# Cross-attention and expert stage: context loaded transposed as well, Wq and Wk folded, keys' low parts on GpSimd

## What is computed

```python
x = x + attention(layernorm(x), ctx)        # ctx: 4 x 1601 x 128
#   Q = ln(x) Wq + bq;  K = ctx Wk + bk;  V = ctx Wv + bv
#   softmax(clip(Q K^T / sqrt(128), -100, 100)) V
x = x + experts(layernorm(x))               # 8 experts, hidden 256, top 2 by router
```

## Time and profile before

| | us |
|---|---|
| median of 3 runs | 165.13 |
| lowest, highest | 164.04, 165.61 |
| span of the profiled execution, first to last instruction | 162.5 |

### The profile page before, as it was taken

One profiled execution on the slowest core, in us unless ns is written; L12 is line 12 of the kernel. 1 busy time (PEld: TensorE's weight loads), 2 busy tenths in 40 slices (PEclk: granted clock), 3 DMA queues, 4 the chain that ended last, 5 costly groups with the idle time before them and its releaser, 6 DMA issues. The chain is left out here.

```text
span 162.5 us, 2919 instructions
## 1 busy us (share of the span) xinstructions
PE 153.8 (95%) x932; PEld 134.7 (83%) x932; DVE 126.0 (78%) x330; ACT 105.9 (65%) x215; POOL 35.8 (22%) x36
## 2 busy tenths in 40 slices
PE   7779999999999999999999989989999999999983
PEld 7569887889989989888869867778888888887872
DVE  0789996496976578177387799899899979977794
ACT  3178785747484636727586745788798798888550
POOL 1292000000120030010063670333323323333020
PEclk9999999999999999999999999999999999999999
DMA  4999960000000000000000000000000000000022
GB/s 134 266 404 376 386 223 0 0 0 2 4 0 0 0 0 4 0 2 0 4 0 0 0 0 4 0 0 0 4 4 0 0 0 0 0 0 0 0 69 65
DMA packets 5188, 7.92 MB, mean 49 GB/s; under 512 B 300, under 2 KB 3000, under 8 KB 5176
## 3 DMA queue, kind: packets, MB, share of 16 engines
q1 hardware_dynamic: 5032, 7.63, 13.8%
q10 hardware_dynamic: 144, 0.13, 0.3%
HBM read 7.24 MB, written 0.52 MB: 48 GB/s over the span
## 5 line engine op out<-in xcount | busy, mean ns | idle before, releaser
L371 ACT ACTIVATE pT<-T 128x512 f32<-128x512 f32 (+1 forms) x28 | 15.4, 565 | 19.7 <-PE T L991 19.5
L918 PE MATMUL S<-x_hi,w_hi 128*128 128x512 f32 x64 | 27.0, 421 | 0.9 <-DVE gate L789 0.9
L1003 PE MATMUL O<-pT,ctx_sb 128*128 128x256 f32 (+1 forms) x104 | 26.5, 381 | 0.2 <-ACT pT L371 0.2
L303 POOL TENSOR_TENSOR x<-x,xn 128x512 f32<-128x512 f32 x13 | 17.8, 1370 | 38.1 <-ACT xn L467 38.0
L441 ACT ACTIVATE gate<-gate 128x512 f32<-128x512 f32 x32 | 20.1, 630 | 8.8 <-DVE gate L789 8.6
L920 PE MATMUL S<-x_hi,w_lo 128*128 128x512 f32 x64 | 25.4, 397 | 0.0
L919 PE MATMUL S<-x_lo,w_hi 128*128 128x512 f32 x64 | 25.2, 394 | 0.0
L435 ACT ACTIVATE up<-S,gub_sb 128x512 f32<-128x512 f32 x32 | 21.9, 686 | 5.1 <-PE S L920 4.7
L789 DVE TENSOR_SCALAR gate<-S,more_sb 128x512 f32<-128x512 f32 x32 | 23.6, 739 | 1.3 <-PE S L920 1.3
L266 POOL TENSOR_TENSOR rstd<-ve,minus_half 128x2 f32<-128x2 f32 (+1 forms) x7 | 7.1, 1008 | 71.9 <-DVE ve L621 66.2
L795 DVE TENSOR_SCALAR up<-up 128x512 f32<-128x512 f32 x32 | 18.3, 574 | 4.9 <-ACT up L435 4.4
(11 more groups left out here) (117 smaller groups left out, 261.1 us busy)
## 6 DMA issues: line engine op xcount, KB each, us to landing
ctx_sb<-in_ctx SPq DMA_DIRECT2D x3, 768.0 KB
gu_sb<-in_gu SPq DMA_DIRECT2D x1, 2048.0 KB, 13.6
ctx_sb<-in_ctx SPq DMA_DIRECT2D x1, 512.0 KB
x_sb<-in_x SPq DMA_DIRECT2D x1, 384.0 KB, 3.9
ctx_sb<-in_ctx SPq DMA_DIRECT2D x1, 256.0 KB, 5.5
out_x<-xn SPq DMA_DIRECT2D x1, 256.0 KB, 2.3
out_x<-xn SPq DMA_DIRECT2D x2, 128.0 KB, 1.8
ctx_sb<-in_ctx SPq DMA_DIRECT2D x4, 32.5 KB
```

Source lines behind the costliest of these rows:

```text
L303: nc.gpsimd.tensor_tensor(acc, acc, y_sb[:, k % 2, :], ALU.add).then_inc(y_added, 1)
L918: nc.tensor.matmul(dst, a_hi, b_hi, start=True, stop=False)
L1003: ins = nc.tensor.matmul(O[:, 0:TPB * P], ctx_sb[b][0:rows, t, :], pT[0:rows, t, :], start=(t == 0), stop=(t == KT - 1))
```

## The change

The host also hands over the context transposed, padded to 1,602 columns. Batch 0's comes in four chunks, the others in one transfer each into two raw buffers (`ct_raw`). No context is transposed on PE. ACT copies the raw keys to `ct_hi`: four chunks for batch 0 (`split_first`), one instruction of 1,602 columns for each later batch (`split_keys`). The low parts of batch 0 are subtracted by DVE, those of batches 1 to 3 by POOL, one instruction of 1,602 columns each. Wq and Wk are multiplied once (`fold_weights`, with three columns for the biases), so that g comes from xT in one product, with the bias added on eviction; the query projection and its eviction are gone. The limits of clipping get a constant part (`find_clip_ends`). All three pieces are prepared before batch 1. x's larger part is issued by ACT. The buffers `gate` and `up` of the expert stage now lie in those of raw keys and scores.

Transfers, and POOL:

```diff
+            def keys_transposed(b):
+                if b >= 2:
+                    sp.wait_ge(ct_lo_ready, NCH + b - 2)
+                sp.dma_start(ct_raw[b % 2], ctxT_in[b]).then_inc(ctT_in_s[b - 1], 16)
...
-            sp.dma_start(x_sb[:, TPB:TILES], x_v[:, TPB:TILES]).then_inc(x1_in, 16)
-            for b in range(BATCHES):
-
...
+            for c, (c0, _, w) in enumerate(SCORE_CHUNKS):
+                sp.dma_start(ct_raw[0][:, c0:c0 + w], ctxT_in[0][:, c0:c0 + w]).then_inc(ctT_first_in[c], 16)
+            keys_transposed(1)
+            keys(0)
+            sp.dma_start(rows_sb[:], rows.partition_broadcast(P)).then_inc(rows_in, 16)
+            sp.dma_start(more_sb[:], more_w).then_inc(more_in, 16)
+            keys_transposed(2)
+            keys(1)
             sp.dma_start(gu_sb[:].rearrange("p (e n) -> p e n", e=EXPERTS), gu.rearrange("e h n -> h e n")).then_inc(gu_in, 16)
+            keys_transposed(3)
+            keys(2)
+            keys(3)
...
-            for b in range(BATCHES):
+            for b in range(1, BATCHES):
+                pool.wait_ge(ct_hi_ready, NCH + b)
+                nc.gpsimd.tensor_tensor(ct_lo[b % 2][:], ct_raw[b % 2], ct_hi[b % 2][:].bitcast(F32),
+                                        ALU.subtract).then_inc(ct_lo_ready, 1)
+                if b == 2:
+                    inverse_root(rstd2[:, 0:TPB], ve2[:, 0:TPB], TPB, var2_ready, 1, rstd2_ready)
+            for b in range(1, BATCHES):
                 s = slice(b * TPB, (b + 1) * TPB)
                 inverse_root(rstd2[:, s], ve2[:, s], TPB, var2_ready, b + 1, rstd2_ready)
```

ACT:

```diff
+            act.dma_start(x_sb[:, TPB:TILES], x_v[:, TPB:TILES]).then_inc(x1_in, 16)
...
+            def split_keys(b):
+
+                act.wait_ge(ctT_in_s[b - 1], 16)
+                if b >= 2:
+                    act.wait_ge(s_done, (b - 1) * TPB * NCH)
+                nc.scalar.activation(ct_hi[b % 2][:], ct_raw[b % 2], ACT.Copy).then_inc(ct_hi_ready, 1)
...
+            copy_fold()
+            split_first(0)
             copy_xT(0)
-            split_ctx(0, 0)
-            evict_q(0)
-            split_ctx(0, 1)
+            split_first(1)
             split_g(0)
-            split_ctx(0, 2)
-            split_ctx(0, 3)
+            split_first(2)
+            split_first(3)
             normalise(1)
+            copy_xT(1)
+            split_keys(1)
+            split_g(1)
             normalise(2)
-            copy_xT(1)
-            split_ctx(1, 0)
-            split_ctx(1, 1)
-            evict_q(1)
             exponentials(0, 0)
-            split_ctx(1, 2)
-            split_ctx(1, 3)
-            split_g(1)
-            split_ctx(2, 0)
-            split_ctx(2, 1)
+            copy_xT(2)
+            split_g(2)
             exponentials(0, 1)
+            split_keys(2)
...
                 if b + 2 < BATCHES:
-                    split_ctx(b + 2, 0)
-                    split_ctx(b + 2, 1)
+                    split_keys(b + 2)
```

DVE, PE, and the host:

```diff
+            def split_first(c):
+                c0, _, w = SCORE_CHUNKS[c]
+                dve.wait_ge(ct_hi_ready, c + 1)
+                nc.vector.tensor_tensor(ct_lo[0][:, c0:c0 + w], ct_raw[0][:, c0:c0 + w],
+                                        ct_hi[0][:, c0:c0 + w].bitcast(F32), ALU.subtract).then_inc(ct_lo_ready, 1)
+
+            def find_clip_ends():
+
+                dve.wait_ge(fold_ready, 1)
+                nc.vector.tensor_scalar(clip_ends[:, 0:1], row_const, -1.0, CLIP, ALU.mult, ALU.add)
+                nc.vector.tensor_scalar(clip_ends[:, 1:2], row_const, -1.0, -CLIP, ALU.mult, ALU.add).then_inc(clip_ends_ready, 1)
...
             dve.wait_ge(x0_in, 16)
             moments(x_sb, stats, mv, ve, 0, TPB, var_ready)
+            find_clip_ends()
             normalise(xn, x_sb, mv, rstd, 0, TPB, rstd_ready, 1, xn_ready)
-            dve.wait_ge(att_in, 16)
-            nc.vector.tensor_scalar(bqs_sb[:], bqk_sb[:, 0:1], SCALE, None, ALU.mult).then_inc(bq_scaled, 1)
+            split_first(0)
             dve.wait_ge(x1_in, 16)
-            for j in range(1, len(PREP)):
-                t0, n = PREP[j]
-                moments(x_sb, stats, mv, ve, t0, n, var_ready, neg_mean)
-            split_ctx(0, 0)
-            split_ctx(0, 1)
+            moments(x_sb, stats, mv, ve, *PREP[1], var_ready, neg_mean)
+            split_first(1)
+            dve.wait_ge(clip_ends_ready, 1)
             split_g(0)
-            split_ctx(0, 2)
-            split_ctx(0, 3)
+            split_first(2)
+            split_first(3)
             clip_scores(0, 0)
             finish_scores(0, 0)
-            split_ctx(1, 0)
-            split_ctx(1, 1)
+            moments(x_sb, stats, mv, ve, *PREP[2], var_ready, neg_mean)
+            split_g(1)
             clip_scores(0, 1)
-            split_ctx(1, 2)
-            split_ctx(1, 3)
-            split_g(1)
+            split_g(2)
             finish_scores(0, 1)
```

```diff
+                    pe.wait_ge(fold_ready, 1)
...
+            def fold_weights():
+
+                pe.wait_ge(att_in, 16)
+                nc.tensor.matmul(M[:, 0:DIM], wqT_sb, wkT_sb, start=True, stop=True)
+                nc.tensor.matmul(M[:, DIM:DIM + 1], wqT_sb, bk_sb, start=True, stop=True)
+                nc.tensor.matmul(M[:, DIM + 1:DIM + 2], wkT_sb, bq_sb, start=True, stop=True)
+                nc.tensor.matmul(M[:, DIM + 2:DIM + 3], bq_sb.to_broadcast([P, P]), bk_sb, start=True,
+                                 stop=True).then_inc(fold_done, 1)
...
+            fold_weights()
             transpose_xn(0)
-            transpose_ctx(0, 0)
-            project_q(0)
-            transpose_ctx(0, 1)
             fold_keys(0)
-            transpose_ctx(0, 2)
-            transpose_ctx(0, 3)
...
             scores(0, 0, range(NCH))
             transpose_xn(1)
-            transpose_ctx(1, 0)
-            transpose_ctx(1, 1)
-            project_q(1)
+            fold_keys(1)
             scores(0, 1, range(NCH))
-            transpose_ctx(1, 2)
-            transpose_ctx(1, 3)
-            fold_keys(1)
+            transpose_xn(2)
+            fold_keys(2)
             for b in range(1, BATCHES):
-                if b + 1 < BATCHES:
-                    transpose_ctx(b + 1, 0)
-                    transpose_ctx(b + 1, 1)
-
-
                 scores(b, 0, [0, 1])
                 if 2 <= b < BATCHES - 1:
                     project_v(b - 2)
@@ -1073,22 +1048,13 @@
                     transpose_p(b - 1, 0)
                     transpose_p(b - 1, 1)
                 scores(b, 0, [3])
-                if b + 1 < len(PREP):
...
                 sum_part(b - 1, 0)
-                if b + 1 < len(PREP):
-                    project_q(b + 1)
-                if b + 1 < BATCHES:
-                    transpose_ctx(b + 1, 2)
-                    transpose_ctx(b + 1, 3)
                 if b >= 2:
                     transpose_x2(b - 2)
                 scores(b, 1, range(NCH))
-                if b + 1 < len(PREP):
-                    fold_keys(b + 1)
```

```diff
+    ctxT = np.zeros((BATCHES, DIM, KEYS_EVEN), np.float32)
+    ctxT[:, :, 0:KT_FULL * P] = (np.asarray(ctx_1024)[:, 0:KT_FULL * P].reshape(BATCHES, P, KT_FULL, DIM)
+                                 .transpose(0, 3, 2, 1).reshape(BATCHES, DIM, KT_FULL * P))
+    ctxT[:, :, KT_FULL * P:KEYS] = np.asarray(ctx_1024)[:, KT_FULL * P:].transpose(0, 2, 1)
```

More of the change, by code:

```diff
@@ L54 @@
 PREP = [(0, 2), (2, 3), (5, 3)]
-CTX_GROUPS = [(t, min(4, KT - t)) for t in range(0, KT, 4)]
 PT_GROUPS = [(t, min(2, KT - t)) for t in range(0, KT, 2)]
-CTX_FIRST = 4
 PAIRS = EXPERTS // 2
@@ L68, in _transpose_bank_uses, with build @@
 def _transpose_bank_uses():
-    order = [("ctx", 0, g) for g in range(len(CTX_GROUPS))]
-    for b in range(BATCHES + 1):
-        for ctx_part, pt_part in (((0, 1), (0, 1, 2, 3)), ((2, 3), (4, 5, 6))):
-            order += [("ctx", b + 1, g) for g in ctx_part if b + 1 < BATCHES]
-            order += [("pt", b - 1, g) for g in pt_part if b >= 1]
     seen, found = [0, 0], {}
-    for kind, b, g in order:
-        found[kind, b, g] = (g % 2, seen[g % 2])
-        seen[g % 2] += 1
+    for b in range(BATCHES):
+        for g in range(len(PT_GROUPS)):
+            found[b, g] = (g % 2, seen[g % 2])
+            seen[g % 2] += 1
     return found, seen
 T_USE, T_TOTAL = _transpose_bank_uses()
-def build(nc, x, ctx_in, att_w, more_w, rows, gu, dn, db, out):
+def build(nc, x, ctx_in, ctxT_in, att_w, more_w, rows, gu, dn, db, out):
     es = ExitStack()
@@ L138, in build @@
         ct_lo = [sb(f"ct_lo{i}", [P, KEYS_EVEN], F32R) for i in range(2)]
+        ct_all = sb("ct_all", [P, 2 * KEYS_EVEN])
+        ct_raw = [ct_all[:, i * KEYS_EVEN:(i + 1) * KEYS_EVEN] for i in range(2)]
         sc = sb("sc", [P, TPB, KEYS_EVEN])
@@ L769, in _ @@
                 clip_scores(b, 1)
-                if b + 1 < len(PREP):
-                    split_g(b + 1)
                 if b >= 2:
```

149 lines of the change are left out of this document (52 added, 97 removed).

## The result

| | before | after |
|---|---|---|
| median, us (4 runs each, same chip) | 165.3 | 169.95 |
| lowest, highest | 164.04, 165.61 | 169.16, 170.86 |
| ratio after to before, 95% interval | | 1.031 (1.024 to 1.038) |
| span of the profiled execution | 162.5 | 167.5 |
| its own time | not given | 169.23 |

A forecast was written before the change was run, and what follows sets the result against it. PE's own work bounds the kernel to about 80 us. Start -0.6, chain making it +3.9 in all, removed work -3.1 and -0.6 (the latter filled by the wait), collision +3.4: +3.65, span 166.15, plus 2.63: 168.8 us, own range 167.5 to 170.0.

The forecast's parts named there:

- PE's own work: PE sets the pace up to about 80 us; transposes and query projection go from it.
- the 6.8 us: Work taken off PE: 5.1 us of context transposes and 1.7 of query projection; the gain if PE stayed full.
- The start: Up to batch 0's first scores: they come at 10.8 instead of 11.42 us, 0.6 early.
- The chain: DVE, POOL, ACT and PE links between batches 0 and 1: first weighted sum at 28.9 to 29.1, not 25.15 us.
- 3.9 us late: PE's delay at the first weighted sum, between batches 0 and 1, in spite of the work removed.
- GpSimd's pass: POOL's low part of a later batch's keys, 1,602 columns: 3.63 us; batch 1's runs 20.5 to 24.2, its scores start at 24.3.
- The collision: Batch 2: xn2 on DVE waits for POOL's ct_lo(3) at their shared port; costs 3.4 us, bounds zero and 4.0.
- The warning on idle gaps: Skill page cited for rival 3: a long idle gap puts TensorE back to half rate.
- The sum: Start, chain, removed PE work and collision: span up 3.65 to 166.15; 2.63 carried over gives 168.8 us.
- 1 (no collision): At POOL's root of batch 2, xn2 gets ahead of ct_lo(3) or needs no port; 165.3 us; chance 0.20.
- 2 (PE stays full): Chain from moments to first copy is shorter; most of 6.8 us arrives, down to 159 us; chance 0.15.
- Rival 3: Collision plus PE at half rate after idling, 13 to 29 us and at 46; some 2 us, 170.8; chance 0.10.

The follow-up runs named there:

- e3: Changed kernel plus 28 unread 128-column matmuls in PE's idle places up to the start of batch 1; 168.24 us, 1.022 to the kernel before.
- e1: Changed kernel with POOL's low part of batch 3 waiting until DVE has written xn2 of batch 0; 166.46 us, 1.015 to the kernel before.
- e2: Changed kernel with POOL's low part of batch 3 in place but as four instructions of some 400 columns; 167.83 us, 1.023 to the kernel before.
- e5: Kernel before the change plus one POOL pass of 1,602 columns beside the normalisation of batch 0's x2; 170.03 us, 1.034 to the kernel before.
- e4: Changed kernel with DVE taking the third piece's moments ahead of the first split of g; 169.47 us, 1.032 to the kernel before.
- e8: Changed kernel with e1's wait, 36 extra matmuls and ACT's first two pT copies ahead of splitting batch 2's keys; 163.82 us, 0.996 to the kernel before.
- e9: e8 with its 36 extra matmuls taken out and nothing else; 167.30 us, 1.013 to the kernel before.
- e11: e7 with tile (0,1) scores finished earlier, batch 1's low part halved, p transposed earlier, six fewer extra matmuls; 162.18 us, 0.982 to the kernel before.
- e7: Changed kernel with low parts on DVE, e4's moments, 32 extra matmuls and e8's ACT order; 163.40 us, 0.994 to the kernel before.

## Why the prediction was right, point by point

- **PE's own work.** The page's 151.3 us of busy PE hold stretches at half rate, so they say nothing direct on the 6.8 us. Where the clock was full the gain shows: from the first weighted sum to the scores of batch 2 it is 9.68 us, and 13.15 before, 3.5 less; forecast 3.1.
- **The start.** 11.59, not 10.8. The order was right (the limits wait for the copy, xn stands behind them), the sizes were not: xn ended near 7.6 as forecast, but from the fold matmul at 8.64 to the scores it took 2.95 us, where I had carried over 2.16. Some 0.6 of the difference is the fold and its columns, partly at half rate (1.53 us from 8.64, where it was 0.93, and 1.04 in e3 at full rate), the rest three DVE instructions that got longer with their new operands (0.21 each for the limits, before 0.15).
- **The chain.** Each link is there; the first sum at 31.31 and not near 29. The missing 2.3 us are the half rate: the twelve score matmuls of tile (0,0) took 4.17 us, at 0.18 apart 2.2; those of tile (1,0) were slow as well. With the clock held (e3) the same order gave 28.84. So the term "3.9 us late" was right for a PE at full rate, and the step that failed inside a forecast that came true was to give the slower level a chance of 0.10, and a place at 46 us. It fell at 9.0 and 26.1 us, behind sparse stretches, and not in the stand of 2.6 us at 48 (clock 1.00 there).
- **GpSimd's pass.** 3.63 us was too much for batches 1 and 3: 3.06 and 3.02. For batch 2 it was 3.64. A price per element from 512 and 1,024 columns did not carry over. That the pass for batch 1 decides the start of the scores of batch 1 was right (24.2 and 24.3 forecast, 26.05 and 26.15 measured).
- **The collision.** The place, the mechanism and the victim as forecast: 2.8 us by e1 against 3.4, the difference being the size of the pass. The Trainium skill (SBUF — State Buffer, section SBUF: two separate sides) has the pair of ports held exclusively for an instruction; e1, e2 and e5 agree, with 3.0 us for 1,602 columns in the changed kernel and 3.6 in e5. What I didn't see was the second meeting at 30.9 (DVE 4.46 us). It hit no instruction that PE needed soon, and neither did the held cast in e3 and e4.
- **The warning on idle gaps.** The Trainium skill (TensorE: Matmul & The Clock Gate, section Why this matters for your kernels) was cited for one long gap. The runs agree that keeping the engine fed pays: e8 against e9, 1.7%. What they show beyond it is that no long gap is needed: both falls of the changed kernel came behind idle places of 1.4 us and less. A stand of 2.6 us in an otherwise full stretch was followed by no fall, nor was the one of 3.4 us in e5's trace.
- **The sum.** Forecast span 166.15, measured 167.5: the clock adds 2.3; PE gained 0.4 more behind the first sum than forecast, and the collision cost 0.6 less, which leaves the 1.3. The time over the span was carried over at 2.63 and is 1.73 in the profiled execution; in later runs of the kernel before it is 2.0 (164.3 and 162.3), so the median had been set beside a span that was not its own, and the base was some 0.6 too high. So 168.8 against 169.23 there, and 169.95 for the median, rests partly on errors that cancel. That the median still lies in the forecast's own range, by 0.05 us, is luck: the 2.3 us of the clock stood nowhere in the sum.
- **Rivals.** 1 (no collision) and 2 (PE stays full) fell. Rival 3's mechanism, the slower level, came true beside the forecast's, at another place and with 2.3 us for its 2, and the time of 169.95 lies between 168.8 and its 170.8.

Of the 3.1%, then: 1.6 points are the collision (e1) and 1.7 the clock (e8 against e9), together a little more than the loss, and both gone leaves the kernel at 0.996. That the rest of the work taken off PE is under the chain of the first batch is borne out by e11, whose shorter chain gets 1.2 points more than e7.
